# A causal mask moved from a matrix product to VectorE's maximum, and six tile scalings moved to GpSimd, in the attention stage of a fused kernel

## The reference

```python
def _L1_attn_ref(x, w_qkv, w_o):            # 32 heads of 16, 8 key/value heads
    qkv = x @ w_qkv
    ...
    keys = jnp.repeat(xk, N_REP, axis=1)
    values = jnp.repeat(xv, N_REP, axis=1)
    scores = jnp.einsum('bhsd,bhtd->bhst', xq, keys) * scale
    causal = jnp.tril(jnp.ones((seq, seq), dtype=bool))[None, None]
    scores = jnp.where(causal, scores, -jnp.inf)
    probs = jax.nn.softmax(scores, axis=-1)
    out = jnp.einsum('bhst,bhtd->bhsd', probs, values)
    ...
x = x + _layernorm(_L1_attn_ref(_layernorm(x), ...))
x = x + _layernorm(_L1_ffn_ref(_layernorm(x), ...))   # x @ W.T + bias, W by a table
```

## Time and profile before

| | |
|---|---|
| median of 3 runs | 1717.28 us (1716.76 to 1717.55) |
| the profiled execution | 1716.84 us, of which its span, first to last instruction, 1715.0 us |
| busy in the span | PE 1608.0 us (94%), PEld 1351.1 (79%), DVE 1093.8 (64%), ACT 739.1 (43%), POOL 494.9 (29%) |
| units of the attention | 192, from about 1188 to 1669 us |
| mean granted TensorE clock | 0.982 |

### The profile page before, as it was taken

The page is one execution under the profiler, slowest core; times in us unless marked ns, Lnnn a source line. Parts: engine busy times, 40 slices in busy tenths (PEclk is TensorE's granted clock), DMA queues, the critical chain, the costliest instruction groups (busy, mean ns, idle before and its releaser), DMA issues. The chain is left out here.

```text
span 1715.0 us, 25191 instructions
## 1 busy us (share of the span) xinstructions
PE 1608.0 (94%) x8661; PEld 1351.1 (79%) x8661; DVE 1093.8 (64%) x2325; ACT 739.1 (43%) x1619; POOL 494.9 (29%) x596
## 2 busy tenths in 40 slices
PE   4999999999999999999999999995899999999994
PEld 4899887888888888877887888784788888888883
DVE  6888778435466554666334322464888888888884
ACT  3766575222332322222122222222776676776770
POOL 4456455211111111443111111343213322322321
PEclk8999999999999999999999999997999999999997
DMA  3000002000010101232001111212323213312300
GB/s 137 25 13 26 1 26 66 19 25 18 28 42 29 36 25 41 74 112 71 16 22 41 32 32 31 80 56 85 99 57 112 81 58 97 99 51 87 117 2 25
DMA packets 67137, 89.85 MB, mean 52 GB/s; under 512 B 8320, under 2 KB 38176, under 8 KB 67008
## 3 DMA queue, kind: packets, MB, share of 16 engines
q1 hardware_dynamic: 67008, 88.22, 16.9%
HBM read 68.27 MB, written 19.92 MB: 51 GB/s over the span
## 5 line engine op out<-in xcount | busy, mean ns | idle before, releaser
L1281 POOL TENSOR_TENSOR m_a_lo<-m_prod,m_a_hi 128x512 fp32r<-128x512 f32 x100 | 134.9, 1349 | 632.6 <-ACT m_a_hi L1363 632.5
L1516 DVE TENSOR_TENSOR m_prod<-m_prod,a_ps 128x512 f32<-128x512 f32 x100 | 68.8, 688 | 383.4 <-ACT m_prod L1357 383.4
L1357 ACT ACTIVATE m_prod<-a_ps 128x512 f32<-128x512 f32 x100 | 59.9, 599 | 544.5 <-PE a_ps L128 544.5
L2083 ACT ACTIVATE t_p<-a_ps,t_nmax 128x128 f32<-128x128 f32 (+1 forms) x512 | 181.3, 429 | 34.3 <-DVE t_nmax L2189 33.2
L2195 DVE TENSOR_TENSOR t_pT_lo<-a_ps,t_pT_hi 128x512 fp32r<-128x512 f32 x192 | 132.1, 688 | 35.0 <-ACT t_pT_hi L2076 33.3
L2189 DVE TENSOR_REDUCE t_nmax<-a_ps 128x2 f32<-128x512 f32 (+1 forms) x192 | 130.7, 681 | 24.5 <-PE a_ps L2282 20.0
L2076 ACT ACTIVATE t_pT_hi<-a_ps 128x512 fp32r<-128x512 f32 x192 | 116.5, 607 | 64.3 <-PE a_ps L2293 62.8
L128 PE MATMUL a_ps<-m_hT_hi,m_w_lo 128*128 128x512 f32 x312 | 123.9, 397 | 0.0
L126 PE MATMUL a_ps<-m_hT_hi,m_w_hi 128*128 128x512 f32 x312 | 123.2, 395 | 0.7 <-DVE f_w_lo L1421 0.7
L127 PE MATMUL a_ps<-m_hT_lo,m_w_hi 128*128 128x512 f32 x312 | 123.3, 395 | 0.0
L2293 PE MATMUL a_ps<-consts,t_p 128*128 128x128 f32 x768 | 117.5, 276 | 0.7 <-ACT t_p L2083 0.7
(11 more groups left out here) (290 smaller groups left out, 4431.0 us busy)
## 6 DMA issues: line engine op xcount, KB each, us to landing
m_raw<-in_w_mlp SPq DMA_DIRECT2D x75, 256.0 KB, 2.7
t_qT<-q_store SPq DMA_DIRECT2D x128, 128.0 KB, 3.0
q_store<-t_qh SPq DMA_DIRECT2D x16, 512.0 KB, 3.0
t_kT<-k_store SPq DMA_DIRECT2D x128, 64.0 KB, 2.3
a_xt<-in_x SPq DMA_DIRECT2D x8, 512.0 KB, 3.8
t_yl<-in_x SPq DMA_DIRECT2D x16, 256.0 KB, 4.0
x_store<-stream SPq DMA_DIRECT2D x4, 1024.0 KB, 5.2
t_yl<-x_store SPq DMA_DIRECT2D x16, 256.0 KB, 2.8
```

What stands on the lines that cost most here:

```text
L1281: pool.tensor_tensor(a_lo[:, n % 2, :], prod[:, :], f(a_hi[:, n % 2, :]), ALU.subtract).then_inc(lo, 1)
L1516: dve.tensor_tensor(prod[:, :], prod[:, :], ps[:, U + TURN_AT["unit", n, 0] % 2, :], ALU.mult).then_inc(prodd, 1)
L2083: last = act.activation(p[:, u % 2, h * width:(h + 1) * width], unit_bank(u)[:, h * width:(h + 1) * width], ACT.Exp, bias=nmax[:, u % 3, h ...
```

## The change

PE no longer multiplies by the mask. DVE's `maximum` becomes one tensor_tensor_reduce per head: it adds a mask from SBUF (now 256 columns wide, zeros and then the triangle) to the head's scores, multiplies by -1, writes that back into the PSUM bank, and gives the minimum of it into `nmax`. ScalarE takes the exponential with a scale of -1. The normalisation for the job "x" moves from DVE's slots 1 and 3 to GpSimd's, behind `roots`. The scalings of `yo` and `yl` move from DVE to GpSimd, just before the add that follows them there, for all batches but the last. `id_r` is gone; `mask` is plain fp32 of twice the width.

```diff
-    def normalise(dve, k, t, b):
+    def normalise(eng, k, t, b):
...
-        dve.tensor_scalar(xf[:, t, :], stream[:, i, :], mv[:, n, t, 0:1], rs[:, n, t:t + 1],
+        eng.tensor_scalar(xf[:, t, :], stream[:, i, :], mv[:, n, t, 0:1], rs[:, n, t:t + 1],
                           ALU.subtract, ALU.mult).then_inc(xn if k == "x" else hn, 1)
+
+    def scale(eng, t, b, k, y, before, done):
+        i, n = tile(t, b), SETS.index(k)
+        eng.wait_ge(root[k], i + 1)
+        eng.wait_ge(before, i + 1)
+        eng.tensor_scalar(y[:, t, :], y[:, t, :], mv[:, n, t, 0:1], rs[:, n, t:t + 1], ALU.subtract, ALU.mult)\
+           .then_inc(done, 1)
@@ gpsimd_program
             if n == 0:
                 if in_batch(b + 1):
                     roots(pool, "x", 1, b + 1)
+            if n in (1, 3) and in_batch(b + 1):
+                normalise(pool, "x", n // 2, b + 1)
...
             for _, t, batch in AT["o_add"].get(s, ()):
                 if batch != BATCH - 1:
+                    scale(pool, t, batch, "o", yo, y_out, o_scaled)
                     o_add(t, batch)
...
             for _, t, batch in AT["e_add"].get(s, ()):
                 if batch != BATCH - 1:
+                    scale(pool, t, batch, "e", yl, y_biased, e_scaled)
                     e_add(t, batch)
@@ scalar_program
                 last = act.activation(p[:, u % 2, h * width:(h + 1) * width],
-                                      unit_bank(u)[:, h * width:(h + 1) * width], ACT.Exp, bias=nmax[:, u % 3, h:h + 1])
+                                      unit_bank(u)[:, h * width:(h + 1) * width], ACT.Exp, scale=-1.0,
+                                      bias=nmax[:, u % 3, h:h + 1])
...
-        act.activation(id_r[:, :], ident, ACT.Copy).then_inc(masks, 1)
-        act.activation(mask[:, :], consts[:, C_MN:C_MN + P], ACT.Copy).then_inc(masks, 1)
+        act.activation(mask[:, 0:P], ident, ACT.Copy, scale=0.0).then_inc(masks, 1)
+        act.activation(mask[:, P:SEQ], consts[:, C_MN:C_MN + P], ACT.Copy).then_inc(masks, 1)
@@ vector_program
         def maximum(u):
-            heads = 4 if u % 3 == 0 else 2
+            heads, width = (4, P) if u % 3 == 0 else (2, SEQ)
             dve.wait_ge(sc, u + 1)
             wait(dve, ex, u - 2)
-            dve.tensor_reduce(nmax[:, u % 3, 0:heads], unit_bank(u).rearrange("p (h t) -> p h t", h=heads),
-                              AX, ALU.max, negate=True).then_inc(mx, 1)
+            if u == 0:
+                dve.wait_ge(masks, 2)
+            for h in range(heads):
+                at = unit_bank(u)[:, h * width:(h + 1) * width]
+                last = dve.tensor_tensor_reduce(at, at, mask[:, SEQ - width:SEQ], -1.0, 1e30, ALU.add, ALU.min,
+                                                accum_out=nmax[:, u % 3, h:h + 1])
+            last.then_inc(mx, 1)
...
-            if n in (1, 3) and in_batch(b + 1):
-                normalise(dve, "x", n // 2, b + 1)
...
             for _, t, batch in AT["e_add"].get(s, ()):
-                scale(t, batch, "e", yl, y_biased, e_scaled)
                 if batch == BATCH - 1:
+                    scale(dve, t, batch, "e", yl, y_biased, e_scaled)
                     last_e_add(t)
...
             for _, t, batch in AT["o_add"].get(s, ()):
-                scale(t, batch, "o", yo, y_out, o_scaled)
                 if batch == BATCH - 1:
+                    scale(dve, t, batch, "o", yo, y_out, o_scaled)
                     last_o_add(t)
@@ tensor_program, scores(u)
             if r == 0:
                 for h in range(2):
-                    pe.matmul(bank[:, 2 * h * P:2 * (h + 1) * P].rearrange("p (h t) -> p h t", h=2),
-                              qT[:, 2 * g + h, 0:P], kT[:, :, g, 0:P], start=h == 0, stop=False)
-                pe.matmul(bank.rearrange("p (h t) -> p h t", h=4), id_r[:, :],
-                          mask[:, :].unsqueeze(1).broadcast_to([P, 4, P]), start=False, stop=True).then_inc(sc, 1)
+                    mm = pe.matmul(bank[:, 2 * h * P:2 * (h + 1) * P].rearrange("p (h t) -> p h t", h=2),
+                              qT[:, 2 * g + h, 0:P], kT[:, :, g, 0:P], start=h == 0, stop=h == 1)
+                mm.then_inc(sc, 1)
             else:
                 pe.matmul(bank.rearrange("p (h t) -> p h t", h=2), qT[:, 2 * g + r - 1, P:SEQ], kT[:, :, g, :],
-                          start=True, stop=False)
-                pe.matmul(bank.rearrange("p (h t) -> p h t", h=2)[:, :, P:SEQ], id_r[:, :],
-                          mask[:, :].unsqueeze(1).broadcast_to([P, 2, P]), start=False, stop=True).then_inc(sc, 1)
+                          start=True, stop=True).then_inc(sc, 1)
...
-            pe.wait_ge(masks, 2)
...
-    id_r, mask = beside_lora.sb("t_id_r", [P, P], F32R), beside_lora.sb("t_mask", [P, P], F32R)
+    mask = beside_lora.sb("t_mask", [P, SEQ])
```

More of the change, by code:

```diff
@@ L1820, in attention_layer @@
     stats, mv, var, rs, ratio, halves = small
-    hT_hi, hT_lo, kT, v2, id_r, mask, rot, qk, halves_of, qT, nmax, p, pT_hi, pT_lo, oT, rinv, osum, ao = buffers
+    hT_hi, hT_lo, kT, v2, mask, rot, qk, halves_of, qT, nmax, p, pT_hi, pT_lo, oT, rinv, osum, ao = buffers
     yo = xf
@@ L1912, in aggregate @@
         dve.bn_aggr(mv[:, n, t, :], stats[:, n, t, :]).then_inc(agg[k], 1)
-    def normalise(dve, k, t, b):
+    def normalise(eng, k, t, b):
         i, n = tile(t, b), SETS.index(k)
-        h = TURN[k, t, b]
-        dve.wait_ge(root[k], i + 1)
+        eng.wait_ge(root[k], i + 1)
         if k == "x":
-            wait(dve, x_mm, DONE.get(("h", 0, t, b - 3), 0))
+            wait(eng, x_mm, DONE.get(("h", 0, t, b - 3), 0))
         else:
-            wait(dve, o_total, i + 1)
-        dve.tensor_scalar(xf[:, t, :], stream[:, i, :], mv[:, n, t, 0:1], rs[:, n, t:t + 1],
+            wait(eng, o_total, i + 1)
+        eng.tensor_scalar(xf[:, t, :], stream[:, i, :], mv[:, n, t, 0:1], rs[:, n, t:t + 1],
                           ALU.subtract, ALU.mult).then_inc(xn if k == "x" else hn, 1)
+    def scale(eng, t, b, k, y, before, done):
+        i, n = tile(t, b), SETS.index(k)
+        eng.wait_ge(root[k], i + 1)
+        eng.wait_ge(before, i + 1)
+        eng.tensor_scalar(y[:, t, :], y[:, t, :], mv[:, n, t, 0:1], rs[:, n, t:t + 1], ALU.subtract, ALU.mult)\
+           .then_inc(done, 1)
     def first_roots(pool):
@@ L2195, in low @@
             dve.tensor_tensor(pT_lo[u % PT_RING][:, :], unit_bank(u), f(pT_hi[u % PT_RING][:, :]), ALU.subtract).then_inc(pl, 1)
[L2197 to L2202, removed]
         def choose():
@@ L2823, in later_stages @@
     l_hi, l_lo = ([w[:, k, :] for k in range(DT)] for w in lut)
-    buffers = hT_hi, hT_lo, kT, v2, id_r, mask, rot, qk, halves_of, qT, nmax, p, pT_hi, pT_lo, (oT_0, oT_1), rinv, osum, ao
+    buffers = hT_hi, hT_lo, kT, v2, mask, rot, qk, halves_of, qT, nmax, p, pT_hi, pT_lo, (oT_0, oT_1), rinv, osum, ao
     attention = attention_layer(nc, d, consts, stream, heads_store, w_hi, w_lo, l_hi, l_lo, bias[:, :], square, picked, xf, yl,
```

## The result

The changed kernel takes 1737.54 us (median of 4 runs, 1735.74 to 1738.81), the kernel before 1717.41 on the same chip: ratio 1.0116, 95% interval 1.0104 to 1.0129. It is slower by 20 us; the forecast was 1705, and the range ended at 1736. The profiled execution took 1737.07 us, of which the span is 1735.2.

The account below looks back on a forecast made before the run. It took PE to decide in slots 5 to 16 of each batch and DVE in the rest. A middle batch fell from 62.27 to 60.58 us; 7 x 1.69 = 11.8 us off 1717.28 gave about 1705, range 1687 to 1736.

Parts of the forecast that it names:

- part 4: GpSimd takes six tensor_scalars per batch at 1.29 us each, 7.7 us on top of 18.0; only queue latency counts.
- D: Slots 17 to 24 of a middle batch, where DVE decides; forecast to go from 22.46 to 22.9 us.
- part 2: DVE's maximum in pieces costs 0.48 us more per four-head unit and 0.20 more per two-head unit.
- Next tokens: GpSimd's normalisations in slots 1 and 3: the first hidden by 2.3 us, the second about on time; nothing charged.
- B: Slots 5 to 9 of a middle batch, where PE decides; forecast to go from 13.11 to 12.27 us.
- A: Slots 1 to 4 of a middle batch, where DVE decides; forecast to go from 9.83 to 9.11 us.
- `yo` in D: GpSimd's scale and add before DVE's moments: DVE waits 0.2 us, once per batch.
- Part 1: The mask product leaves PE; worth 1.92 us per batch, only in the slots where PE decides.
- a: Cost of the extra result per piece of DVE's maximum; taken as 0.07 us, bounded by 0 and 0.16.
- rival of dear pieces: DVE's maximum, every slot: at 0.16 us extra per piece DVE becomes the bound, 1740 us; chance 0.28.
- Part 3: Six tensor_scalars per batch leave DVE: -1.80 us in A, -0.90 in D.
- GpSimd in DVE's way: DVE's two remaining tensor_scalars and the chain before its moments slow: +1.5 us per batch, about 1715; chance 0.10.

Follow-up runs that it names:

- cheap_steps: The changed kernel with all three kinds of moved GpSimd steps as one tensor_tensor with the root broadcast, mean left out; 1709.32 us, ratio 0.9954.
- x_back: The changed kernel with only the normalisation of the next tokens back on VectorE, slots 1 and 3; 1727.1 us, ratio 1.0059.
- o_back: The changed kernel with only the scaling of `yo` back on VectorE; 1726.3 us, ratio 1.0061.
- mask_only: The changed kernel with the normalisations and scalings back on VectorE, mask and maximum as changed; 1719.37 us, ratio 1.0009.
- x_early_o: The changed kernel with GpSimd normalising next tokens in slots 0 and 1, not 1 and 3, and `yo` scaled on VectorE; 1714.28 us, ratio 0.9983.
- by_stretch: The kernel before, with the changed maximum only for units 6 to 17 of each batch and nothing moved to GpSimd; 1711.89 us, ratio 0.9966.

## Why the prediction was wrong

**The step that failed** is the price in part 4: "I take 1.29, the neighbour's". GpSimd's tensor_scalar with two pointer scalars takes 2.08 us, and the end that I kept for the range, 1.68, did not hold it either. The rows that bounded it were tensor_tensors; a row of the same operation at that size was not there, and I treated the operation as if its kind did not matter. With it two waits failed that were put at nothing and at 0.2 us (below). cheap_steps has the steps at 1.04, below my 1.29, and there the batch takes 61.07 us for a forecast of 60.58, and the kernel 1709 for 1705. That the rest comes so near is partly luck, as D and part 2 show. By its own last sentence the prediction was wrong in kind, since PE does wait for `xn`.

**Next tokens, "I charge nothing".** The reasoning had the second tile start when the root of the last layer's tile 1 is out. At 2.08 us the root itself was late, since the first tile, a scale and an add stood before it in GpSimd's queue: 2.08 + 2.08 + 1.28 in a row. That is a wait of 2.05 us for PE per batch, and B 2.9 over its forecast (15.14 for 12.27). Against x_back's 12.09 it is 3.1: 1.5 us is the work that PE could not do in A, and 1.6 the lower granted clock behind the wait (o_back), a cost that the prediction did not have at all; over the five batches that show it, 1.6 is an estimated 8 of the 20 us. The ending of the prediction named the sign, PE waiting for `xn` in slot 4.

**`yo` in D.** The chain was named and its place was right; the wait was sized at 0.2 us once per batch, and is 1.13 for one tile, most of it the 0.79 by which the scale is dearer, and 0.46 for the other. D is 24.43 for 22.9. The chain is 1.10 of that: cheap_steps, with the cheap scale, has 23.33. The other 0.43 is a step of the sum. DVE idled for 2.28 us in D before (22.46 less 20.18), and the prediction carried on only 0.94 of it, dropping 1.34 without a reason. In cheap_steps DVE is busy for 21.07 us in D and idles for 2.26, as much as before.

**Part 1.** Right where it said it would pay: B fell by 0.99 in mask_only (forecast 0.84), C by 0.50. The forecast for C, 16.3, was met (16.37) by two errors that cancel: PE fell only to 16.09 busy, not 15.70, and DVE rose only to 15.27, not 16.02.

**Part 2.** a is 0.05 or less for 0.07. The rival of dear pieces (a over 0.10, chance 0.28) is refuted, though it had the time nearly right: 1740 for 1737.5. The measured time alone would have spoken for a wrong cause; the pieces' starts and mask_only tell them apart. The price of 0.07 hid other misses: a is about 0.035 on average (0.15 in four pieces, 0.06 in two), and by the prediction's own rates that takes 0.35 from A and 0.77 from D, which gives 8.8 and 22.1. cheap_steps has 9.28 and 23.33, so with the right a the forecast would have been further off.

**Part 3.** Six tensor_scalars were to give 2.7 us per batch; in A, where four of them are, the change has 9.29 and mask_only 10.25, so 0.96 for 1.80. What holds A at 9.3 no run here separates: it takes 9.29 us in the change, where PE is busy for 7.21 of them, and 9.28 in cheap_steps, where PE has 8.94. In D the two scalings bring 0.23 (23.56 in mask_only, 23.33 in cheap_steps) for 0.90.

**GpSimd in DVE's way** did not happen: DVE's tensor_scalar at L1922 takes 534 ns on average in the change, for 535 before. The third rival had the chain before the moments in it, but as an extra of 0.4 us.

**What the half weights hid.** 65.22 - 62.27 is 2.95 per batch, times 7 is 20.7; the median moved by 20.1. That is partly luck. By the ends of `low` in the two profiles, the six middle batches together lose 15.1 us (one of them, the first, has no wait in B), the two short ones 2.4, and the time behind the last unit 2.6 (48.3 for 45.8), where the scaling of `yl` stands in GpSimd's queue and the prediction had nothing.

## What to carry to other kernels

A step moved to an idle engine is paid in latency, not in load: follow that engine's queue with the new durations up to the next instruction that somebody waits for, and place the step where its inputs are long known (x_early_o: the same work one and two slots earlier, 12 us). Price an operation on another engine by a row of the same operation there; if there is none, let the range reach well beyond the nearest (here the step cost 1.6 times its neighbour), or use the form that a row shows. And where different engines decide in different stretches, make such a trade only in the stretches that it pays in (by_stretch).

## What was not expected of the hardware

On GpSimd a tensor_scalar of 128x512 fp32, one input, two pointer scalars and two operations, takes 2.08 us, and a tensor_tensor with a broadcast column 1.04, so two of the latter cost what one of the former does. The Trainium skill (GPSIMD Engine Reference, section on engine selection) has one-input operations at roughly line rate and two-input ones about twice as slow as VectorE's. Here the one-input form is the dearer one even for a single multiplication, 1.58 us against 1.04 (and 1.28 for an add of two full tiles), and the form with two operations takes 3.9 times VectorE's 535 ns. The reading of VectorE's accumulator costs 0.05 us behind a piece, though its own row says 0.14. And after PE's idle 2.05 us the granted clock was at 0.50 between 1448 and 1450, with PE at work: a wait can cost again when it is over. In o_back the same wait costs B 1.5 us without the lower clock and 3.1 with it.
